# The last pass of a graph network on one core: norms a turn later, squares on ScalarE, and the branch over the general path inside the pass

## The reference

```python
edge_index = stack([src, dst])
x = layernorm(x + L0(x, edge_index, ...))
x = layernorm(x + L1(x, src, dst, edge_attr_16, ...))
```

## Time and profile before

| | us |
|---|---|
| median of 3 runs (1122.97 to 1124.8) | 1123.96 |
| the profiled execution's own time | 1125.9 |
| its span, first to last instruction | 1122.5 |
| PE busy | 938.9 (84% of the span) |
| DVE busy | 701.9 (63%) |
| ACT busy | 391.2 (35%) |
| start of the last pass | 967.6 |
| last product of the last pass ends | 1090.5 |
| last output issued | 1112.8 |

### The profile page before, as it was taken

How to read it: one execution, slowest core, us unless ns; L and a number is a source line. 1 busy time by engine, 2 the same in 40 slices (tenths; PEclk the granted TensorE clock), 3 DMA queues, 4 the chain that set the end, 5 groups by cost and what they waited for, 6 DMA issues and landing times. The chain is left out here.

```text
span 1122.5 us, 19146 instructions
## 1 busy us (share of the span) xinstructions
PE 938.9 (84%) x7566; PEld 573.1 (51%) x7566; DVE 701.9 (63%) x1328; ACT 391.2 (35%) x750; POOL 128.3 (11%) x150
## 2 busy tenths in 40 slices
PE   0358868977877849989999999998899996999982
PEld 0357768877777745535555444444334442444440
DVE  5997899999999625514434765554556563333443
ACT  1675688888876611100000010214202105100000
POOL 4212224233322220000000000000000000000001
PEclk9968988989999969989999999998989998999995
DMA  6534556666666348953775526845037745057730
GB/s 168 88 118 150 179 186 204 210 194 195 191 183 180 134 176 303 355 212 146 313 296 185 215 109 268 317 181 230 15 134 308 284 165 214 19 227 274 270 142 18
DMA packets 65300, 217.59 MB, mean 194 GB/s; under 512 B 29095, under 2 KB 43227, under 8 KB 51667
## 3 DMA queue, kind: packets, MB, share of 16 engines
q1 hardware_dynamic: 55588, 164.52, 41.3%
q0 software_dynamic: 9616, 51.78, 13.2%
HBM read 170.69 MB, written 45.57 MB: 193 GB/s over the span
## 5 line engine op out<-in xcount | busy, mean ns | idle before, releaser
L1398 PE MATMUL PM<-Aring,Xop 128*128 128x512 fp8e4 (+1 forms) x1960 | 397.2, 363 | 1.1 <-issue 1.1
L1398 PEld LDWEIGHTS PM<-Aring,Xop 128*128 128x128 f16 x1960 | 182.4, 98 | 213.9 <-issue 11.4
L837 PE MATMUL PW<-Aring 128*128 128x52 fp8e4 (+3 forms) x2151 | 117.8, 217 | 60.1 <-ACT F L905 57.2
L837 PEld LDWEIGHTS PW<-Aring 128*128 128x128 fp8e4 x2151 | 111.8, 103 | 64.3 <-ACT F L905 59.9
L1398 PE MATMUL PM<-Ares,Xop 128*128 128x512 fp8e4 x588 | 138.7, 391 | 2.9 <-ACT Xop L1974 1.4
L1935 ACT ACTIVATE F<-PH,bag 64x512 f32<-64x512 f32 (+1 forms) x39 | 25.7, 659 | 289.2 <-PE PH L1624 288.7
L1765 DVE TENSOR_SCALAR S<-PM 128x256 f32<-128x256 f32 (+1 forms) x75 | 31.4, 418 | 103.8 <-issue 37.4
L1398 PEld LDWEIGHTS PM<-Ares,Xop 128*128 128x128 f16 x588 | 56.7, 101 | 71.9 <-issue 10.1
L1547 POOL DMA_DIRECT2D out<-dd x12 | 9.1, 757 | 687.5 <-DVE dd L1727 687.5
L905 ACT ACTIVATE F<-PW 128x392 uint16<-128x392 f32 x196 | 84.2, 514 | 9.0 <-PE PW L837 7.8
L695 DVE TENSOR_TENSOR Aring<-Ares 128x4096 uint16<-128x4096 uint16 x31 | 70.8, 2285 | 5.7 <-PE PW L837 5.3
(11 more groups left out here) (158 smaller groups left out, 1172.1 us busy)
## 6 DMA issues: line engine op xcount, KB each, us to landing
Aring<-adj SPq DMA_DIRECT2D x72, 1568.0 KB, 9.9
adj<-Aring POOLq DMA_DIRECT2D x12, 1568.0 KB, 6.8
adj<-Xop POOLq DMA_DIRECT2D x12, 1568.0 KB, 7.0
Ares<-adj SPq DMA_DIRECT2D x6, 1568.0 KB, 21.5
rc<-ea_sum SPq DMA_DIRECT2D x36, 128.0 KB, 4.6
Aring<-adj SPq DMA_DIRECT2D x4, 784.0 KB, 4.6
rc<-rc_d SPq DMA_DIRECT2D x12, 256.0 KB, 9.9
eaf<-in_erow SPq DMA_DIRECT2D x60, 51.0 KB, 2.4
```

The costliest lines, as they stand in the source:

```text
L837: last = nc.tensor.matmul(PW[begun % RING][:, c:c + 52 * (z - y)].rearrange("p (d v b) -> p d v b", d=z - y, b=2), lo[:, h % 2, i, :].bitc ...
L1398: last = nc.tensor.matmul(o, x[:, h, :], rhs, start=h == 0, stop=h == NT - 1)
```

## The change

Only the fast path's last pass changes in what is executed. The diff, cut to that:

```diff
-        for p in range(5):
+        for p in range(4):
             with nc.Block() as block:
...
+        def closing(engine, slowly, tail):
+
+            engine.wait_ge(t["s_flag"], 1)
+            wrong = engine.value_load(m["flag"][0:1, 0:1], min_val=0, max_val=1)
+            with engine.If(wrong == 1):
+                tail()
+                for k, part in enumerate(slow):
+                    slowly(part, engine)
+                    meet(engine, k)
+            with engine.Else():
+                tail()
+
         with nc.Block() as block:
-            @block.sync
-            def _(sp):
-                wrong = sp.value_load(m["flag"][0:1, 0:1], min_val=0, max_val=1)
-                with sp.If(wrong == 1):
-                    for k, part in enumerate(slow):
-                        part.run_sync(sp)
-                        meet(sp, k)
...
+            propagate(nc, ins, m, t, 4, pick(0), out, lambda: [*sets[1].values()], block, closing)
```

```diff
+        if closing:
+            for b in range(8):
+                write(b)
+            closing(g, lambda part, engine: part.run_gpsimd(engine), lambda: written(8))
...
+        def centred(b):
+
+            n, P = tiles(b)
+            x = R[0:P, 4 * b:4 * b + n, :]
+            s = stt[0:P, b % 2]
+            v.wait_ge(s_g, b + 1)
+            nc.vector.tensor_tensor(x, PG[b % 2][0:P, 0:n, 0:64], x, ALU.add).then_inc(s_v, 1)
+            v.wait_ge(s_v, b + 1)
+            own(nc.vector.tensor_reduce(s[:, 0, 0:n], x, AX.X, ALU.add))
+            if b >= 2:
+                v.wait_ge(s_o[b % 2], 16 * (b // 2))
+            nc.vector.scalar_tensor_tensor(dd[0:P, b % 2, 0:n, :],
+                                           s[:, 0, 0:n].rearrange("p (n o) -> p n o", o=1).broadcast_to([P, n, 64]),
+                                           -1.0 / 64, x, ALU.mult, ALU.add).then_inc(s_a, 1)
+
+        def scaled(b):
+
+            n, P = tiles(b)
+            d, s = dd[0:P, b % 2, 0:n, :], stt[0:P, b % 2]
+            v.wait_ge(s_a2, b + 1)
+            own(nc.vector.reciprocal(s[:, 1, 0:n], s[:, 3, 0:n]))
+            nc.vector.tensor_tensor(d, d, s[:, 1, 0:n].rearrange("p (n o) -> p n o", o=1).broadcast_to([P, n, 64]),
+                                    ALU.mult).then_inc(s_gd, 1)
...
-                v.wait_ge(s_g, b + 1)
-                nc.vector.tensor_tensor(R[0:P, c, :], pg[:, :, 0:64], R[0:P, c, :], ALU.add).then_inc(s_v, 1)
-                v.wait_ge(s_v, b + 1)
-                norm(b, P, n, True).then_inc(s_gd, 1)
+                centred(b)
+                if b < NB - 5:
+                    scaled(b)
+                elif b > NB - 5:
+                    scaled(b - 1)
+                if b == NB - 1:
+                    scaled(b)
...
-        lag = 1 if p == 1 else 2
-        for i in range(NB + lag + 1):
+        lag = {1: 1, 4: 3}.get(p, 2)
+
+        def turn(i):
...
+        for i in range(NB - 1 if closing else NB + lag + 1):
+            turn(i)
+        before = k[0]
+        if closing:
+            closing(v, lambda part, engine: part.run_vector(engine), tail)
...
-    def root(b):
+    def root(act, b):
         n, P = tiles(b)
+        act.wait_ge(s_a, b + 1)
+        for j in range(n):
+            nc.scalar.activation(sq[0:P, b % 2, j, :], dd[0:P, b % 2, j, :], ACT.Square,
+                                 accum_out=stt[0:P, b % 2, 2, j:j + 1]).then_inc(s_sq, 1)
+        act.wait_ge(s_sq, 4 * b + n)
         nc.scalar.activation(stt[0:P, b % 2, 3, 0:n], stt[0:P, b % 2, 2, 0:n], ACT.Sqrt, bias=EPS,
                              scale=1.0 / 64).then_inc(s_a2, 1)
...
+        if closing:
+            for b in range(NB - 3):
+                turn(b)
+            closing(act, lambda part, engine: part.run_scalar(engine), lambda: tail(NB - 3))
```

More of the change, by code:

```diff
@@ L1060, in layers @@
             "s_rd": sem("s_rd"),
+            "s_flag": sem("s_flag"),
         }
@@ L1081, in layers @@
         once = [x for x in t.values() if type(x) is type(t["s_mm"])]
-        slow = [*restart(nc, ins, m, t, [*sets[0].values(), *sets[1].values(), *once]), Stage()]
+        slow = [Stage(), *restart(nc, ins, m, t, lambda: [*sets[0].values(), *sets[1].values(), *once]), Stage()]
         general(nc, ins, m, t, -1, pick(2), slow[-1])
@@ L1106, in meet @@
                 engine.drain()
-        with nc.Block() as block:
-            @block.sync
-            def _(sp):
-                wrong = sp.value_load(m["flag"][0:1, 0:1], min_val=0, max_val=1)
-                with sp.If(wrong == 1):
-                    for k, part in enumerate(slow):
-                        part.run_sync(sp)
-                        meet(sp, k)
[L1117 to L1147, removed]
+        def closing(engine, slowly, tail):
[8 more added lines that the diff above has]
+                tail()
+        with nc.Block() as block:
+            propagate(nc, ins, m, t, 4, pick(0), out, lambda: [*sets[1].values()], block, closing)
 class Stage:
@@ L1179, in _ @@
         g.dma_reset()
-        for one in used:
+        for one in used():
             g.sem_clear(one)
@@ L1400, in multiply, with propagate @@
         last.then_inc(t["s_mm"], 1)
-def propagate(nc, ins, m, t, p, sem, out, past, block):
+def propagate(nc, ins, m, t, p, sem, out, past, block, closing=None):
     F, R, Xop, Xnew = m["F"], m["R"], m["Xop"][p % 2], m["Xop"][(p + 1) % 2]
@@ L1422, in propagate @@
     s_a2 = sem("a2")
[L1423 to L1428, removed]
+    if p == 1:
+        s_t, s_te = sem("t"), sem("te")
+    if p == 4:
+        s_o, s_tot, s_told, s_sq = [sem("o0"), sem("o1")], sem("tot"), sem("told"), sem("sq")
     mm0 = NB * max(0, p - 1)
@@ L1524, in _ @@
                 factors(b + 2)
+        if closing:
+            closing(sp, lambda part, engine: part.run_sync(engine), lambda: None)
     @block.gpsimd
@@ L1550, in write, with written @@
                 g.dma_start(out[b * 512:N, :], dd[0:TAIL, b % 2, 0]).then_inc(s_o[b % 2], 16)
[L1552 to L1557, removed]
+        def written(first):
+            for b in range(first, NB):
+                write(b)
             g.wait_ge(s_o[0], 16 * 7)
             g.wait_ge(s_o[1], 16 * 6)
+        if closing:
+            for b in range(8):
+                write(b)
+            closing(g, lambda part, engine: part.run_gpsimd(engine), lambda: written(8))
+        elif slow:
+            for b in range(NB + 3):
+                if b < NB:
+                    hand_over(b)
+                if p == 4 and 3 <= b < NB:
+                    write(b - 3)
+            if p == 4:
+                written(NB - 3)
     def landed(engine, b):
@@ L1699, in _ @@
             ahead(36, NT)
+        if closing:
+            closing(pe, lambda part, engine: part.run_tensor(engine), lambda: None)
     @block.vector
@@ L1709, in own, with norm @@
             v.wait_ge(s_own, k[0])
-        def norm(b, P, n, final):
+        def norm(b, P, n):
             x = R[0:P, 4 * b:4 * b + n, :]
@@ L1719, in norm @@
             own(nc.vector.tensor_single_scalar(s[:, 1, 0:n], s[:, 0, 0:n], -1.0 / 64, ALU.mult))
-            if final and b >= 2:
-                v.wait_ge(s_o[b % 2], 16 * (b // 2))
             own(nc.vector.tensor_tensor(d, x, wide(s[:, 1, 0:n]), ALU.add))
@@ L1726, in norm @@
             own(nc.vector.reciprocal(s[:, 1, 0:n], s[:, 3, 0:n]))
-            return nc.vector.tensor_tensor(d if final else x, d, wide(s[:, 1, 0:n]), ALU.mult)
+            return nc.vector.tensor_tensor(x, d, wide(s[:, 1, 0:n]), ALU.mult)
+        def centred(b):
[18 more added lines that the diff above has]
+                                    ALU.mult).then_inc(s_gd, 1)
         def by_quad(x):
@@ L1812, in tell @@
                 own(nc.vector.tensor_reduce(fl[:, 13:14], fl[:, 8:13], AX.X, ALU.min))
-                own(nc.vector.tensor_single_scalar(m["flag"][:, 0:1], fl[:, 13:14], 0.5, ALU.is_lt))
+                nc.vector.tensor_single_scalar(m["flag"][:, 0:1], fl[:, 13:14], 0.5,
+                                               ALU.is_lt).then_inc(t["s_flag"], 1)
         def rest(b):
@@ L1837, in rest @@
                 v.wait_ge(s_v, b + 1)
-                norm(b, P, n, False).then_inc(s_gd, 1)
+                norm(b, P, n).then_inc(s_gd, 1)
                 v.wait_ge(s_gd, b + 1)
@@ L1877, in _, with tail @@
                 tell(i)
+        def tail():
+            k[0] = before
+            for i in range(NB - 1, NB + lag + 1):
+                turn(i)
+        for i in range(NB - 1 if closing else NB + lag + 1):
+            turn(i)
+        before = k[0]
+        if closing:
+            closing(v, lambda part, engine: part.run_vector(engine), tail)
         if p in (2, 3):
@@ L1910, in _, with turn @@
     def _(act):
-        for b in range(NB):
+        def turn(b):
             for r, (q, blocks) in enumerate(ROUNDS):
@@ L1931, in _ @@
                 if p == 4 and b % 2 == 0 and 2 <= b < NB - 1:
-                    act.wait_ge(s_a, b - 1)
-                    root(b - 2)
```

(16 more changed lines are left out.)

1 line of the change is left out of this document (removed).

## The result

The changed kernel takes 1111.04 us (median of 4, 1110.47 to 1114.11) against 1124.38 us for the kernel before on the same chip; the ratio is 0.988, with a 95% interval of 0.986 to 0.991. Measured again later beside two other kernels it was 0.987 (0.984 to 0.990). The forecast was 1112.7 us in a range of 1110.6 to 1117.0.

What follows compares the result with a forecast made beforehand. PE bounds the kernel up to 1090.5 us, leaving the 32.0 us after it; 4.9 (tail) plus 6.5 (end), less 0.1, takes 11.3 us off the profiled execution, putting the median at 1112.7 us, range 1110.6 to 1117.0.

Steps and rivals of the forecast that it cites:

- The end, 6.5 us: After the last landing: branches moved into the pass leave 1.45 us in place of 7.95, if the fetches are hidden.
- PE's last couple: Blocks 10 and 11 on PE: start at 1090.6 instead of 1093.38 (2.8 us), full clock 1.90 instead of 3.68 (1.8 us).
- DVE's branch "with no margin": Behind DVE's turn 11: fetch 5.0 us, back at 1088.1, product 11 ready since 1087.25; PE waits perhaps 0.1 us.
- rival 1: DVE comes back late from its branch inside the pass; chance 0.14.
- The squares: Moved from DVE to ACT: four 64-wide squares at 0.38 us each, 1.75 us with the root; DVE loses about 1.1.
- rival 3: ACT reloads its tables at each root, two loads or 2.57 us; output 12 lands at 1116.6, time 1119.6 us; chance 0.04.
- The prediction's bound of 1.02 us each: Upper bound for ACT's squares, as the 832-wide: still hidden but for the last, +0.6 us.
- What is late next: In the tail, block b's fused subtraction waits for output b-2 (two buffers of d): period 3.8 us, DVE idle 1.5 to 2.5.
- Some 5 us sooner without it: In the tail: without the 3.8 us period of waits on outputs, the last output would land some 5 us sooner.
- Rival 2: Pass's arm ends in a jump to code not held; last barrier waits 5.0 us again, 1117.7 us; chance 0.08.
- Rival 4: DVE's fetch in the pass is served behind other transfers, up to 16.3 us; about 1125.8 us, slower; chance 0.02.
- The tail's sum: From the pass's tail to the span's end: 4.9 plus 6.5 is 11.4, less 0.1 for PE's wait, 11.3 us.

Runs made afterwards that it cites:

- the branch alone one turn earlier: Changed kernel with old norm, lag 2 and squares on DVE; branches inside the pass, DVE's behind turn 10: tail 28.84 us, median 1114.87 us, ratio 0.992.
- lag and squares only: Changed kernel with the branches in a block of their own behind the pass, as before: tail 28.96 us, median 1118.12 us, ratio 0.996.
- branch inside only: Changed kernel with the old norm, lag 2 and squares on DVE; DVE's branch behind turn 11: tail 32.47 us, median 1120.05 us, ratio 0.997.
- mixed: Changed kernel with four buffers of d, outputs 8 to 10 issued by POOL, 11 and 12 by SP: tail 16.36 us, median 1104.11 us, ratio 0.981.

## Why the prediction was right, point by point

- **The end, 6.5 us:** 6.45 by the changed kernel's own rows, 6.4 by the branch alone one turn earlier, and 5.5 against the kernel with lag and squares only, whose fetch at the end was shorter. That the stall goes with the branch is shown by the three kernels with DVE's branch in other places: it costs nothing where DVE has time to spare, and shows on the path where it has none. The kernel with no branch shows that nothing of it is left in the changed one.
- **PE's last couple:** predicted 2.8 + 1.8 us. Relative to product 11 it starts at 3.23 instead of 6.13, 2.9 us earlier, and its first four matmuls take 1.01 us; ACT starts on the result 1.90 us after the couple's start, as forecast (3.68 before). The 0.1 us that PE was to wait does not appear. The sum took it off twice, as the walk through the tail already starts PE at 1090.6; it should have said 11.4.
- **DVE's branch "with no margin": wrong, on the safe side.** Two terms were too large. ACT's squares and root took 1.33 us up to the reciprocal's start (1077.83 to 1079.16), not 1.75. And the fetch took 3.1 us, not 5.0. The flag load (1079.4) ran beside the multiply (1079.37), as the walk had it. For the fetch I had one sample, taken where five engines fetch at once; the ten profiles here with DVE's branch in the pass show 2.8 to 3.2 us behind it, and 3.4 to 5.2 as PE's branch is listed. So DVE is back 1.7 us before product 11 ends, and rival 1 was less likely than its 0.14.
- **The squares:** predicted 0.38 each from the pair of 832 wide, measured 0.24 (1088.85 to 1089.11 for the first pair, 0.24 from there on). The accumulator read overlaps the next ACTIVATE. The fused subtraction took 0.43, near the 0.42 taken; the upper bound of 0.68 was the 512-wide update of F, whose row is not among. No table was loaded in the pass, so rival 3 is out. The prediction's bound of 1.02 us each was read wrongly: four squares and the root would then take 4.35 us, more than the round of 3.8, and cost some 0.5 us in every turn of the tail and not only in the last.
- **What is late next:** right as put. Waits of 1.98, 1.98 and 2.40 us were inside the 1.5 to 2.5 forecast, and the round is 3.74 us twice and then 3.55, against 3.8. "Some 5 us sooner without it" compares with 4.6 for the tail and 6.0 for the last issue in the kernel with four buffers.
- **Rival 2** (the stall stays) is out: the drain follows the landing. **Rival 4** needed a fetch of some 14.5 us at DVE's branch, against 3.1.
- **The tail's sum:** 11.3 forecast, 11.8 measured: 5.3 us up to the last landing (27.3 us after product 11 before, 22.0 now), where the sum had 4.9, and 6.45 behind it. The median fell by 13.3 in the first comparison and by 13.9 in the second. What lies beyond 11.8 isn't explained by the pass; in the profiled pair 2.0 us of the span are the earlier end of product 11, and the barrier that ends the first pass came at 477.0 before and at 474.2 with the change, so that lead arose ahead of it, in the part that builds the matrix or in the first pass. Behind that barrier nothing is added to it. The scatter there was the term mis-sized: I took 1 us, while the start of the tail spreads over 9 us across these executions, and the runs of the kernel before lie between 1117.8 and 1128.7. That the median came within 1.7 us of the forecast is thus in part luck; the tail is what bears the forecast out. Whether part of the earlier start comes from the change (other places of the code in memory) stays open; no run tells it apart.

## What to carry to other kernels

In these kernels a branch over a long path wasn't paid by its instruction (0.05 to 0.08 us on all engines but PE) but by the pause behind it: 2.8 to 3.2 us on DVE within the pass, 4.1 and 5.0 where all five engines branch at once. With the engine's remaining work in both arms, and the branch where the engine had that much time to spare, it cost nothing. When a stage is lengthened by a step, look at once at the buffers that its output passes through: here the round trip of a store with two buffers took the place of the work that was removed, and two more buffers were worth 4.6 us. An engine that idles in every turn isn't free while its work stands between a landing and the next issue.

## What I had not expected of the hardware

- The pause behind the same branch differs: PE's is listed with 4.9 (before), 3.4 (the change, and lag and squares only), 5.2 (branch inside only) and 5.0 us (DVE's branch a turn later). The changed kernel itself shows 3.4 in one profile and 3.7 in the other. The kernels differ in where their code lies; whether that is the cause was not tried, and it can't be the whole of it.
- POOL's drain behind its last output DMAs takes 1.11 to 1.13 us where it ends the pass, though all of them have landed; in the block of the branches, with no DMA ahead of it, it took 0.11 (before, and lag and squares only).
- An output of 128 KB in rows of 256 bytes lands in 2.38 us alone from POOL, and from SP in 4.26, 3.68, 1.97 and 2.0 us (two buffers), 3.5, 2.0 and 3.7 (four buffers) and 2.3 (mixed). The first two overlap PE's code fetch (branch at 1098.4, listed with 3.9 us) and so does the 3.04 us landing of the kernel with DVE's late branch; but in the changed kernel a landing beside PE's fetch (1095.3 to 1098.7) took 2.38. I can't say what the rule is.
